# Graph kernel with a shared ring of adjacency strips: strips pass in steps of two row groups, and GpSimd loads the narrow ones too

## What is computed

```python
h = max(layernorm(x), 0)
t0 = h; t1 = adj @ t0; t2 = 2 * adj @ t1 - t0; t3 = 2 * adj @ t2 - t1
x = x + t0 @ w[0] + t1 @ w[1] + t2 @ w[2] + t3 @ w[3]        # Chebyshev layer, K = 4
h = max(layernorm(x), 0)
deg = clip(sum(adj, axis=1) + 1, 1)
z = relu(concat([h, (adj @ h + h) / deg]) @ W + b)
out = x + z / max(norm(z), 1e-12)
```

## Time and profile before

| | us |
|---|---|
| median of 3 runs | 2681.09 |
| lowest, highest | 2674.81, 2688.95 |
| the profiled execution, its own time | 2684.29 |
| its span | 2682.5 |
| TensorE matmul busy | 2150.1 (80%) |
| VectorE busy | 1637.2 (61%) |
| GpSimd busy | 1268.9 (47%) |
| ScalarE busy | 678.8 (25%) |
| data moved by DMA | 690 MB, mean 257 GB/s |

### The profile page before, as it was taken

One profiled execution on the slowest core, in us unless ns is written; L12 is line 12 of the kernel. 1 busy time (PEld: TensorE's weight loads), 2 busy tenths in 40 slices (PEclk: granted clock), 3 DMA queues, 4 the chain that ended last, 5 costly groups with the idle time before them and its releaser, 6 DMA issues.

```text
span 2682.5 us, 29450 instructions
## 1 busy us (share of the span) xinstructions
PE 2150.1 (80%) x12008; PEld 1661.5 (62%) x12008; DVE 1637.2 (61%) x1306; ACT 678.8 (25%) x1667; POOL 1268.9 (47%) x1357
## 2 busy tenths in 40 slices
PE   1578887878999998898659977787668898988785
PEld 1245555656777776787557865565556676765553
DVE  5477666635666654565445555564446766679985
ACT  2334233223222323621111244331101222200000
POOL 4455555344544434732235525334223656657771
PEclk9789999989999999999879998898889999999887
DMA  9699889668877766965467777667655989989995
GB/s 284 218 329 326 301 288 315 231 225 280 286 272 254 252 219 168 302 207 217 172 243 259 233 221 209 200 203 253 222 198 173 336 287 360 332 260 354 365 272 162
DMA packets 220745, 690.06 MB, mean 257 GB/s; under 512 B 47554, under 2 KB 78274, under 8 KB 220610
## 3 DMA queue, kind: packets, MB, share of 16 engines
q0 software_dynamic: 163840, 652.30, 71.3%
q1 hardware_dynamic: 51776, 34.64, 4.9%
q10 hardware_dynamic: 4994, 1.25, 0.3%
HBM read 685.97 MB, written 2.10 MB: 257 GB/s over the span
## 4 chain that ended last, share of the span: by engine, by line
PE 44%; POOL 18%; ACT 11%; DMA 10%; DVE 9%; issue 9%; ACTq 0%; POOLq 0%; DVEq 0%
PE ps_pair L800 32%; POOL ring L395 18%; ACT ring L443 11%; DMA ring<-in_adj_dram,index 9%; DVE ring L652 7%; PE ps_single L806 7%; PE ps_lin L742 1%; PE ps_lin L745 1%; PE ps_single L704 1%; PE ps_tr L761 0%; DMA res<-in_x_dram 0%; PE ps_late L715 0%; PE ps_lin L744 0%; ACT vec_t L454 0%; PE ps_xt L694 0%
## 5 line engine op out<-in xcount | busy, mean ns | idle before, releaser
L652 DVE STREAM_TRANSPOSE ring<-ring 128x2048 f32<-128x2048 f32 (+1 forms) x680 | 1430.8, 2155 | 887.9 <-ACT ring L443 714.7
L395 POOL DMA_INDIRECT ring<-in_adj_dram,index x1344 | 1267.4, 943 | 1356.4 <-PE ps_single L806 503.2
L800 PE MATMUL ps_pair<-ring,vec 128*128 128x256 f32 x5760 | 1349.1, 395 | 258.6 <-DVE ring L652 243.6
L800 PEld LDWEIGHTS ps_pair<-ring,vec 128*128 128x128 f32 x5760 | 1128.4, 198 | 466.9 <-issue 142.1
L806 PE MATMUL ps_single<-ring,vec 128*64 128x256 f32 x4480 | 575.4, 408 | 237.5 <-DVE ring L652 230.4
L443 ACT ACTIVATE ring<-ring 128x1024 f32<-128x1024 f32 (+7 forms) x736 | 574.6, 784 | 590.3 <-DMA ring<-in_adj_dram,index 569.1
L806 PEld LDWEIGHTS ps_single<-ring,vec 128*64 128x64 f32 x4480 | 329.5, 146 | 454.0 <-DVE ring L652 181.7
L466 ACT ACTIVATE sum_s<-ps_single 128x512 f32<-128x512 f32 x64 | 37.8, 591 | 578.9 <-PE ps_single L806 420.1
L443 ACT ACTIVATION_READ_ACCUMULATOR ring<-ring 128x1 f32 x736 | 138.7, 188 | 0.0
L454 ACT ACTIVATE vec_t<-ps_xt 64x512 f32<-64x512 f32 x32 | 18.7, 583 | 172.2 <-PE ps_xt L694 172.2
L624 DVE TENSOR_TENSOR res<-res,ps_late 128x256 f32<-128x256 f32 x12 | 5.1, 421 | 90.3 <-PE ps_late L715 90.3
(11 more groups left out here) (95 smaller groups left out, 580.0 us busy)
## 6 DMA issues: line engine op xcount, KB each, us to landing
ring<-in_adj_dram,index POOLq DMA_INDIRECT x1344, 7.7
ring<-in_adj_dram SPq DMA_DIRECT2D x160, 96.0 KB, 7.0
ring<-in_adj_dram SPq DMA_DIRECT2D x160, 64.0 KB, 7.9
ring<-in_adj_dram SPq DMA_DIRECT2D x160, 32.0 KB
out_dram<-vec SPq DMA_DIRECT2D x64, 32.0 KB
res<-in_x_dram SPq DMA_DIRECT2D x4, 256.0 KB, 8.0
res<-in_x_dram ACTq DMA_DIRECT2D x4, 256.0 KB, 8.4
tmp<-in_L_gnn_weight_dram ACTq DMA_DIRECT2D x2, 64.0 KB
```

Of the source, the lines that this page charges most:

```text
L395: pool.indirect_dma_start(strip_of(i)[:, g, :], None, adj_q, bass.IndirectOffsetOnAxis(ap=index[:, 0:1], axis=0), element_offset=(QN * (g ...
L652: last = nc.vector.transpose(blocks, blocks)
L800: last = nc.tensor.matmul(ps_pair[n % 2][:, cells], vec[:, CB * J + c, :, :], moving, start=(pair == 0), stop=(pair == pairs - 1))
```

## The change

- `NARROW` is 0: every strip is loaded by GpSimd, eight indirect DMAs each. SyncE keeps only the loads of x and the stores.
- The ring is `[P, GH, RING * UC]`: a strip is a range of columns in each of the eight row groups.
- A strip passes in four steps (`PAIRS`) of two row groups, each with its own load semaphore. ScalarE sums and VectorE turns a step when it has landed, over the strip's whole width (`128x2x(w*128)`).
- TensorE still takes units of two blocks, and waits until all four steps of the strip are turned.
- `ring_places` frees by blocks: a strip can be loaded when the last unit that read each covered block is done, and when the strip six before it has begun.
- The diagonal block is turned in place with the rest, and copied to the spare room by `copy_diagonal` behind the row's last strip. TensorE reads it from the ring.
- VectorE's epilogues are placed by a unit number that is interpolated over the four steps.

```diff
-NARROW = 3
+NARROW = 0
+PAIRS = GH // 2
...
-def ring_places(strips):
-
-    at, places, live = 0, [], []
-    for i, (_, _, _, w) in enumerate(strips):
+def ring_places(strips, units):
+
+
+    done = {(i, J): u + 1 for u, (_, i, Js) in enumerate(units) for J in Js}
+    started = {}
+    for u, (_, i, _) in enumerate(units):
+        started.setdefault(i, u + 1)
+    at, owner, places = 0, [0] * RING, []
+    for i, (_, _, J0, w) in enumerate(strips):
         if at + w > RING:
             at = 0
-        clash = [k for k, lo, hi in live if lo < at + w and hi > at]
-        before = max(clash, default=-1) + 1
-        before = max(before, i - NSEM + 1, places[-1][1] if places else 0)
-        live = [(k, lo, hi) for k, lo, hi in live if k >= before] + [(i, at, at + w)]
-        places.append((at, before))
+        free_at = max(owner[at:at + w] + [started[i - NSEM] if i >= NSEM else 0])
+        owner[at:at + w] = [done[i, J] for J in range(J0, J0 + w)]
+        places.append((at, free_at))
         at += w
...
-        ring = sb("ring", [P, RING * GH * UC])
+        ring = sb("ring", [P, GH, RING * UC])
...
-                        .then_inc(s_wide[wide_strips.index(i) % NSEM], 16)
+                        .then_inc(s_wide[wide_strips.index(i) % NSEM][g // 2], 16)
...
+                    for p in range(steps_of[i]):
+                        act.wait_ge(*loads_of(i, p))
+                        for g in range(GH)[groups_of(i, p)]:
+                            cells = strip_of(i)[:, g, (lo - J0) * UC:(hi - J0) * UC]
+                            last = nc.scalar.activation(cells, cells, ACT.Copy,
+                                                        accum_out=into[:, GH * h + g:GH * h + g + 1])
+                        last.then_inc(s_summed, 1)
...
+            def copy_diagonal(n):
+
+                C = rows[n].C
+                if C > 0:
+                    dve.wait_ge(s_late, C)
+                dve.wait_ge(s_turned, steps_to[first_strip[n + 1]])
...
+                            last = nc.vector.tensor_copy(dst.rearrange("p k (e r) -> p k e r", e=2), src)
+                last.then_inc(s_copied, 1)
...
+            for i, (n, h, J0, w) in enumerate(strips):
+                for p in range(steps_of[i]):
+                    dve.wait_ge(*loads_of(i, p))
                     if i in sum_strips:
-                        dve.wait_ge(s_summed, sum_strips.index(i) + 1)
...
+                        dve.wait_ge(s_summed, sums_to[sum_strips.index(i)] + p + 1)
+                    blocks = strip_of(i)[:, groups_of(i, p), :].rearrange("p g (c q) -> p g c q", q=32)
+                    nc.vector.transpose(blocks, blocks).then_inc(s_turned, 1)
+                    u = units_to[i] + (units_to[i + 1] - units_to[i]) * (p + 1) // steps_of[i]
+                    if rows[n].has_late and i + 1 == first_strip[n + 1] and p + 1 == steps_of[i]:
+                        copy_diagonal(n)
...
-                    pe.wait_ge(s_turned, u + 1)
+                    pe.wait_ge(s_turned, steps_to[i + 1])
+                    if row.has_late and row.C in Js:
+                        pe.wait_ge(s_copied, late_rows.index(n) + 1)
```

More of the change, by code:

```diff
@@ L178, in cheb_sage_kernel @@
     strip_first = [min(u for u, (_, i, _) in enumerate(units) if i == at) for at in range(len(strips))]
-    strip_done = [max(u for u, (_, i, _) in enumerate(units) if i == at) + 1 for at in range(len(strips))]
-    places = ring_places(strips)
-    free_at = [max(strip_done[:before], default=0) for _, before in places]
+    places = ring_places(strips, units)
+    free_at = [free for _, free in places]
     narrow = [w <= NARROW for _, _, _, w in strips]
@@ L185, in cheb_sage_kernel @@
     narrow_strips = [i for i in range(len(strips)) if narrow[i]]
+    steps_of = [1 if narrow[i] else PAIRS for i in range(len(strips))]
+    steps_to = [sum(steps_of[:i]) for i in range(len(strips) + 1)]
+    units_to = [min([u for u, (_, k, _) in enumerate(units) if k >= i], default=n_units) for i in range(len(strips))]
+    units_to.append(n_units)
     sum_strips = [i for i, (n, _, _, _) in enumerate(strips) if rows[n].summed(i - first_strip[n])]
@@ L222, in sums_of @@
         return [i for i in sum_strips if strips[i][0] == n]
+    sums_to = [sum(steps_of[i] for i in sum_strips[:k]) for k in range(len(sum_strips) + 1)]
     extra_rows = [n for n, r in enumerate(rows) if r.sweep > 1 and sums_of(n)]
@@ L294, in strip_of, with loads_of @@
         def strip_of(i):
[L296 to L300, removed]
+            at = places[i][0] * UC
+            return ring[:, :, at:at + strips[i][3] * UC]
+        def loads_of(i, p):
             if narrow[i]:
@@ L436, in sum_rows @@
                     lo, hi = row.summed(i - first_strip[n])
-                    act.wait_ge(*loads_of(i))
                     if row.sweep > 1 and extra_rows.index(n) >= 2:
@@ L626, in late_epilogue @@
                     .then_inc(s_lateadd, 1)
+            def copy_diagonal(n):
[3 more added lines that the diff above has]
+                dve.wait_ge(s_turned, steps_to[first_strip[n + 1]])
+                for i in range(first_strip[n], first_strip[n + 1]):
+                    _, h, J0, w = strips[i]
+                    if J0 <= C < J0 + w:
+                        for c in range(CB):
+                            col = (C - J0) * UC + 32 * c
+                            dst = diagonal(C, c)[:, GH // 2 * h:GH // 2 * h + GH // 2, :]
+                            src = strip_of(i)[:, :, col:col + 32].rearrange("p (k e) r -> p k e r", e=2)
+                            last = nc.vector.tensor_copy(dst.rearrange("p k (e r) -> p k e r", e=2), src)
+                last.then_inc(s_copied, 1)
@@ L796, in _ @@
                             moving = strip_of(i)[:, :, chunk:chunk + 32]
-                            if row.has_late and J == row.C:
-                                moving = diagonal(J, c)[:, GH // 2 * h:GH // 2 * h + GH // 2, :]
                             if row.kind(J) == PAIR:
```

63 lines of the change are left out of this document (19 added, 44 removed).

## The result

Over 4 runs the changed kernel takes 2774.18 us (2773.11 to 2778.92), the kernel before 2680.82 (2674.81 to 2688.95) beside it. The ratio is 1.035, 95% interval 1.032 to 1.038: slower by 93 us, where 2765 was predicted. The profiled execution took 2778.92 us, its span is 2776.9.

The account below looks back on a forecast made before the run. The prediction saw three limits: TensorE's waits in sweep 1, late ring release in the middle, GpSimd's issue at the end. Terms summed to +86 us, 2767 on the median's footing, rounded to 2765; range 2690 to 2825.

Parts of the forecast that it names:

- row start: Rows 2 to 13, sweep 1: TensorE waits for all four strip A instructions behind VectorE's wait, +72 us.
- strip B: Sweep 1, 14 rows: TensorE gets this strip 1.8 us later, after VectorE's four instructions and the epilogue, +25 us.
- strips C and D: Sweep 1: TensorE's remaining work falls short of covering VectorE's turning of these strips in five rows, +12 us.
- sums after a landing, in sweep 1: At the start and strips 34 and 36, most sums go ahead of the last landing, -27 us.
- clock: Sweep 1: slower matmuls behind ten new TensorE waits of 7 to 8 us, +10 us, between 0 and 19.
- sweep 2: Rows 18 to 31 lose 1 to 2 us six times, -8; epilogue ahead of a last step, rows 18 to 20, +6.
- rows 32 to 43: Narrow strips moved to GpSimd's issue, and epilogues in or behind the first strip's last step, +10 us (0 to 30).
- middle: Rows 43 to 59: finer release lets strips load earlier, less new epilogue waits, -31 us (-60 to -10).
- last stretch: From strip 167 on, GpSimd issues 31 strips without a wait, partly offset by a faster last landing, +17 us (+10 to +35).
- rival that GpSimd falls behind there by 36 us: Rows 32 to 43: one strip a row is late by 5 us more than read, total 2800 us, chance 0.12.
- rival of the DMA engines as the bound: At the kernel's end DMA engines set the limit, so moving the issue costs nothing: 2750 us, chance 0.2.
- faster rival: At ScalarE's 46 waits for landings, the steps take sums off the path: 2620 us, chance 0.12.

Follow-up runs that it names:

- e9: The changed kernel with VectorE's late additions moved behind the whole of strip A; 2647.16 us, ratio 0.985 to the kernel before.
- e7: The changed kernel with VectorE waiting for the whole strip's sums before its first step; 3030.46 us, ratio 1.128 to the kernel before.
- e12: The kernel before with strip B's sums ahead of ScalarE's L454 copy in sweep 1; 2589.97 us, ratio 0.965.
- e10: The changed kernel with late additions behind strip A, sweep 1 epilogues behind strip B's steps, and NARROW = 3; 2587.21 us, ratio 0.963 to the kernel before.
- e2: The kernel before with TensorE waiting for a strip's whole run of units; 3275.78 us, ratio 1.079, on a chip where the kernel before takes 3033.
- e1: The changed kernel with VectorE's late additions behind strip A, on a chip where the kernel before takes 3033 us; 3185.53 us, ratio 1.051.

## Why the prediction was right, and where it wasn't

The standing still of TensorE in sweep 1, before (209 us) and after (285), can be taken apart by its places, since each wait stands in the timeline:

| term | forecast | measured |
|---|---|---|
| row start | +72 | +72 (7.0, 7.9 or 6.3 us, against 0.4, 1.3 or 0) |
| strip B | +25 | +24 (9.6 for 7.8, 6.3 for 4.5) |
| strips C and D | +12 | +1 (new waits 5.2, small gaps gone 3.8) |
| sums after a landing, in sweep 1 | -27 | -22 (start to row 1: -12; strip 34: -3; strip 36: -7) |
| clock | +10 | +48 to +50 |
| sweep 2 | -8 and +6 | -5 |
| rows 32 to 43 | +10 | -7 |
| middle | -31 | -38 |
| last stretch | +17 | +19 |

**Row start: right in mechanism and size.** VectorE's wait kept its place, four instructions stand behind it and not one, and e9 shows that setting it behind the strip takes the wait away.

**Clock: this is the mis-sized term.** The prediction took +10 us, between 0 and 19, "since the engine will have worked longer before them". It took its price from 24 records behind strip B's wait (1.75 us) and its times from ten new waits. e9 against the change shows 48 us for sweep 1, over eleven new waits. In rows 3 to 6 each cost 7.1 to 7.3 us, 29 in all, because the first 64 records behind it ran slow; in the other seven 1.5 to 3.8, about 18 in all. So even the cheap ones cost more than the 1 us each that I took, and the dear ones have no row before. Which rows are dear changes from run to run: in e7 it is rows 2, 3, 5 and 6, and row 4 ran its 96 records in 13.7 us. That work before the wait would keep the clock up was argued and isn't borne out: in row 5, 26 us at 1.00 stood ahead of it. The error is outside the bounds that I gave.

**Strip B: right.** The pipelining gains nothing there, since its sums start late and VectorE's four steps and the epilogue follow (394.15 to past 404). e7 shows what the steps hide (6.2 us), e12 that the wait itself was ScalarE's order. **Strips C and D** were priced too high by 11 us: rows 3 and 6 show no wait there, and rows 1, 2 and 4 only 1.7, 2.3 and 1.2 us. **Sums after a landing** gave 22 us in sweep 1, four fifths of the forecast; strip 34 gave 3 and not 6, since its sums came to wait for ScalarE's L468 instead of the landing; TensorE's start came 7.2 us later, as the four instructions demand (6.7 forecast).

**Rows 32 to 43: the sign was wrong.** I priced the narrow strips (+10) and found no gain. e10 shows both: on GpSimd they cost 14 us, so the steps and the release give back about 21 there. The rival that GpSimd falls behind there by 36 us is refuted, though its direction was real.

**Middle: right.** Strip 134's wait went from 19.84 to 12.28 us (9 us of gain forecast, 7.6 measured) and strip 141's is gone. Row 46's new wait cost 9.6 (12.3 for 2.7), where I had 7.

**Last stretch: right, as a sum of two larger parts.** GpSimd's 311 us without a wait are in the trace as forecast. But e10 shows that the narrow strips cost 34 us there, so the rest of the change gave about 15. The rival of the DMA engines as the bound, and with it the prediction's reading of the rule of the Trainium skill, "DMA: Bandwidth & Descriptors", section "Rules for kernel authors" (spreading DMAs over issuing engines saves only issue time), would have made this cost nil. That rival is refuted for the changed kernel (89% busy, 34 us back). The rule as such isn't: issue time is the one thing that it lets spreading save, and issue time was the limit here. In e10 the engines are at 99% again, but GpSimd has no pause either, so that run doesn't test it.

**The faster rival** (sums leave the path, 2620) fell, though its size is of interest: e7 shows that the steps' overlap with the sums is worth 257 us within this kernel. The kernel before has another overlap, TensorE starting with the first unit (e2: 8% longer without it). The change traded one for the other.

**Signs.** Sweep 1 ended at 1154, not near 1120 as I had written: sign (3) was off, by the clock. The other signs came about as named, the last landing 4.7 us behind its issue.

That the sum came within 9 us is luck, since errors nearly cancelled: about +40 from the clock and +5 (landings) against -11 (C, D), -17 (rows 32 to 43), -7 (middle), -3 (sweep 2), -1 (B) and +2 (last stretch). In sweep 1 alone I was 34 us too low.

## What to carry to other kernels

When a hand-over between engines gets coarser, look in the consumer's and the producer's fixed order for waits that stand ahead of the piece: what was hidden behind its first part is then wholly exposed, and moving two instructions past it may be worth more than the change. Price a new wait of TensorE with a range for the slow clock behind it, not with one stretch of matmuls: here waits of 6.3 to 7.9 us cost 1.5 to 7.3 us more, 4.4 on average. And take a change of several parts one at a time: here the release alone was a gain, the steps cost 127 us by one misplaced wait, and the narrow strips on GpSimd cost 43 to 50.

## What the runs showed of the hardware that was not expected

- The same kernel takes 2681 to 2686 us on some chips and 3033 on others, 13% apart, and in e1's trace TensorE there has gaps of 0.4 to 2.4 us with no wait that the profile can name, several in a row of the list. Their cause was not found. Edits need not be worth the same there: e1 is 5.1% slower than the kernel before on such a chip, and the identical kernel (e9) 1.5% faster on another.
- After a wait of 7.86 us TensorE ran 19.5 us of gapless work at a mean clock of 0.60 in row 5; in row 7 the same work after the same wait took 14.2 us at 0.86; after 1.28 us it ran at 1.00. By sweep 1's windows the same 4760 records took 869 us (clock 0.87), 821 (0.92) and 790 (0.97), as the waits between them went.
- An indirect DMA of GpSimd costs 1.25 us from start to start even where it brings one block of 128 columns; 248 of them took 311 us.
